# Splitting a group's x one slot sooner, with a wait for each third, in a float32 graph attention kernel

## What is computed

```python
bias = (adj + adj)[:, None]
q = (x @ Wq.T).reshape(b, n, 12, 32); k = (x @ Wk.T)...; v = (x @ Wv.T + bv)...
scores = jnp.einsum('bqhd,bkhd->bhqk', q, k) * 384 ** -0.5 + bias
row_nonzero = jnp.any(scores != 0, axis=-1, keepdims=True)
p = jnp.nan_to_num(softmax(where(row_nonzero, scores, -inf)))
out = einsum('bhqk,bkhd->bqhd', p, v).reshape(b, n, 384) @ Wo.T + bo
result = layernorm(x + out)
```

## Time and profile before

| | us |
|---|---|
| median of 3 runs | 661.67 (661.62 to 662.46) |
| the profiled execution | 661.33 |
| span of its profile | 659.5 |
| PE busy in the span | 638.3 |
| ACT busy | 517.6 |
| DVE busy | 502.6 |
| POOL busy | 410.4 |

### The profile page before, as it was taken

The page is one execution under the profiler, slowest core; times in us unless marked ns, Lnnn a source line. Parts: engine busy times, 40 slices in busy tenths (PEclk is TensorE's granted clock), DMA queues, the critical chain, the costliest instruction groups (busy, mean ns, idle before and its releaser), DMA issues.

```text
span 659.5 us, 18322 instructions
## 1 busy us (share of the span) xinstructions
PE 638.3 (97%) x6060; PEld 550.3 (83%) x6060; DVE 502.6 (76%) x2319; ACT 517.6 (78%) x1942; POOL 410.4 (62%) x500
## 2 busy tenths in 40 slices
PE   9999999999999999999999999999999999999774
PEld 5788888888888888888888888888888888888673
DVE  4667887877887777887877887777877877877884
ACT  5678887878878788877878878788877878877782
POOL 1557665756756666765766856666765756845662
PEclk9999999999999999999999999999999999999999
DMA  9300312121121210212121131210212111011111
GB/s 306 122 4 9 106 57 105 57 74 44 48 105 58 104 50 19 95 59 104 58 86 41 38 106 58 104 50 29 85 58 105 57 50 36 32 58 58 49 49 49
DMA packets 17951, 45.88 MB, mean 70 GB/s; under 512 B 1984, under 2 KB 7104, under 8 KB 17856
## 3 DMA queue, kind: packets, MB, share of 16 engines
q1 hardware_dynamic: 17424, 44.11, 19.3%
q10 hardware_dynamic: 432, 0.59, 0.3%
HBM read 32.11 MB, written 12.58 MB: 68 GB/s over the span
## 4 chain that ended last, share of the span: by engine, by line
PE 67%; POOL 16%; issue 8%; DVE 7%; ACT 2%; POOLq 0%
PE qk_ps L279 21%; PE vo_ps L357 11%; POOL tree L230 10%; PE vo_ps L311 10%; PE pt_ps L325 9%; PE scores_ps L296 6%; PE att_ps L342 5%; DVE nscores L498 4%; POOL x_t L212 4%; PE pt_ps L332 2%; ACT probs L409 2%; PE scores_ps L369 1%; PE pt_ps L265 1%; POOL x_n L219 1%; DVE att_t L538 1%
## 5 line engine op out<-in xcount | busy, mean ns | idle before, releaser
L409 ACT ACTIVATE probs<-nscores,neg_max 128x128 f32<-128x128 f32 x768 | 296.7, 391 | 3.1 <-DVE neg_max L498 3.1
L498 DVE CUSTOM_DVE_ANT_0 nscores<-scores_ps,adj_n 128x128 f32<-128x128 f32 x768 | 171.6, 286 | 16.0 <-PE scores_ps L296 16.0
L409 ACT ACTIVATION_READ_ACCUMULATOR probs<-nscores,neg_max 128x1 f32 x768 | 146.5, 191 | 0.0
L230 POOL TENSOR_TENSOR tree<-nscores 128x768 f32<-128x768 f32 x64 | 120.2, 1878 | 36.0 <-DVE neg_max L498 36.0
L325 PE MATMUL pt_ps<-ident,probs 128*128 128x128 f32 x768 | 118.7, 277 | 9.2 <-ACT probs L409 7.0
L357 PE MATMUL vo_ps<-w_o,att_t 128*128 128x384 f32 x576 | 116.8, 347 | 0.0
L212 POOL TENSOR_TENSOR x_t<-x_raw,x_t 128x512 fp32r<-128x512 f32 x45 | 58.4, 1300 | 93.5 <-ACT x_t L426 93.5
L311 PE MATMUL vo_ps<-w_v,x_t 128*128 128x384 f32 x576 | 114.1, 342 | 0.0
L325 PEld LDWEIGHTS pt_ps<-ident,probs 128*128 128x128 f32 x768 | 89.8, 140 | 28.9 <-ACT probs L409 7.9
L230 POOL TENSOR_TENSOR tree<-tree 128x384 f32<-128x384 f32 (+1 forms) x128 | 103.8, 811 | 10.0
L279 PE MATMUL qk_ps<-x_t,w_k 128*128 128x512 f32 x405 | 105.4, 404 | 2.6 <-POOL x_t L212 2.6
(11 more groups left out here) (56 smaller groups left out, 808.2 us busy)
## 6 DMA issues: line engine op xcount, KB each, us to landing
x_n<-xn SPq DMA_DIRECT2D x32, 384.0 KB, 3.6
out<-out_n SPq DMA_DIRECT2D x32, 384.0 KB, 2.6
x_raw<-xt SPq DMA_DIRECT2D x15, 768.0 KB, 5.4
adj_n<-adj SPq DMA_DIRECT2D x32, 128.0 KB, 2.0
x_raw<-xt SPq DMA_DIRECT2D x3, 256.0 KB, 5.5
nscores<-wq ACTq DMA_DIRECT2D x3, 192.0 KB, 4.2
nscores<-wk SPq DMA_DIRECT2D x3, 192.0 KB, 5.5
probs<-wv SPq DMA_DIRECT2D x1, 576.0 KB, 6.4
```

Of the source, the lines that this page charges most:

```text
L230: nc.gpsimd.tensor_tensor(tree[:, b % 2, :, 0:width], src[:, :, 0:width], src[:, :, width:2 * width], ALU.add).then_inc(tree_step, 1)
L409: last = nc.scalar.activation(probs[:, b % 2, h], nscores[:, b % 2, h], ACT.Exp, bias=neg_max[:, b % 2, h:h + 1], scale=-1.0, accum_out=ro ...
L498: last = nc.vector.tensor_tensor_reduce(out=nscores[:, half, h], in0=scores_ps[j][:, m * P:(m + 1) * P], in1=adj_n[:, b // 2 % 2, half], s ...
```

## The change

`split_in(b)` gives the third that is split at the end of slot b, on ACT and on POOL: third 0 in slot 3, third 1 in slot 0, third 2 in slot 1, and none in slot 2. The group is the same as before, so each third is split one slot sooner; group 2's first third is split in the iteration b = -1. PE's tile 0 waits for one third ahead of each of its three triples of matmuls, in place of one wait for all three ahead of the first.

```diff
+        def split_in(b):
+
+            g, k = (b + 1) // GRP + 2, (b + 1) % GRP
+            return ((g, k),) if k < KT and g < NG else ()
...
-                if 0 <= b and b % GRP < KT and b // GRP + 2 < NG:
-                    split_x_low(b // GRP + 2, b % GRP)
+                for g, k in split_in(b):
+                    split_x_low(g, k)
...
-                if t == 0:
-                    pe.wait_ge(x_split, KT * g)
                 if tile == 0:
                     pe.wait_ge(first_keys, KT)
                 wait(pe, kept, tile)
                 for k in range(KT):
+                    if t == 0:
+                        pe.wait_ge(x_split, KT * (g - 1) + k + 1)
...
-                if 0 <= b and b % GRP < KT and b // GRP + 2 < NG:
-                    split_x_high(b // GRP + 2, b % GRP)
+                for g, k in split_in(b):
+                    split_x_high(g, k)
```

## The result

| | before | changed |
|---|---|---|
| median of 4 runs, us | 661.64 | 655.78 (654.72 to 656.41) |
| the profiled execution, us | 661.33 | 654.72 |
| span, us | 659.5 | 652.9 |

The ratio is 0.9907, with a 95% interval of 0.9890 to 0.9924: 0.9% faster, where 1.0% was forecast. The time lies in the range (654.2 to 656.8).

A forecast was written before the change was run, and what follows sets the result against it. PE was taken as the bound. 661.33 - 6.4 for 14 stalls removed, with nothing for the added waits, gave 654.9 for the profiled execution; the median, 0.34 higher, should be 655.2 us, range 654.2 to 656.8.

The forecast's parts named there:

- The bound: PE, busy 97% of the span, bounds the kernel; a gain must come from its work or its little idling.
- rival 1: Another wait takes the stall's place at tile 0; half the gain goes, 658.5 us; chance 0.05.
- rival 4: POOL's split is held by something other than its place (load or buffer); time stays 661.7 us; chance 0.02.
- part 1: Splits one slot sooner: the stall at slot 3's tile 0 goes wholly, 14 x 0.46 = 6.4 us; lower end 2.7.
- What is late next: After the stall goes, nothing else stands within 0.46 us; the work moved on ACT and POOL costs nothing.
- ACT's cover: ACT's 1.05 us idle at slot 3's end takes the moved 0.62 us high part, leaving 0.43; cost nothing.
- At the start: Group 2's first third added to ACT at b = -1; copy up to 0.1 us late, taken as 0.
- Part 2: Two more waits in each of 15 tiles 0, 30 in all, long satisfied: cost nothing; upper end 6.0 us.
- rival 2: Waits inside tile 0 cost 0.10 us each (658.2 us) or 0.20 (661.2, no change); chance 0.06.
- rival 3: A wait inside tile 0 drains the weight-load pipe, up to 0.43 us each, 668.1 us, slower; chance 0.02.
- The allowance for the differences between runs: Part of the forecast range: 0.8 us, the difference among the three runs shown.
- the 1.2 us kept for the waits: Part of the forecast range: a small price of tile 0's added waits, up to 0.04 us each.

The follow-up runs named there:

- late_before: The kernel before, with POOL making the last third's low part twice (first copy to an unread scratch buffer): 678.67 us, ratio 1.0265.
- late_after: The changed kernel, with POOL making the last third's low part twice (first copy to an unread scratch buffer): 654.77 us, ratio 0.9904.
- late_thirds: The kernel before with tile 0 waiting for each third alone, plus POOL making the last third's low part twice: 661.31 us, ratio 0.9998.
- part 2 alone: The kernel before with splits left in place, but tile 0 waiting for each third alone: 654.90 us, ratio 0.9912.

## Why the prediction was right

**The bound.** That PE is the bound in every slot held to the hundredth: the period after is four slots of pure PE work, 39.01 as forecast, and the delay put in on purpose (late_before) came out in full. The last third is ready at 282.73 in the changed kernel's trace and tile 0's weights start at 291.01, 8.3 us to spare, as forecast. Rivals 1 and 4 are out: the list of PE's waits has no new name, and slot 3 is as long as slot 1.

**The term of part 1.** 14 x 0.46 = 6.4 us against 6.61 in the profiled executions. Of the three readings of a stall (PE's idle 0.19, the weights' idle 0.43, the difference of like slots 0.46) the last was right. PE's own idle figure would have given 2.7 us, 0.27 us too little for each stall. The ends of matmuls are modelled in the profile and overlap in part; that this is why the figure falls short is likely and was not tested.

**What is late next.** Nothing, as forecast. ACT's cover at the new place was 1.05 us and 0.53 of it remain (I had said 0.43); POOL's row sums kept their place with 0.26 us left of 1.29. In late_after the same idle time ahead of slot 2's row sums was used up, and no time was lost. At the start, ACT's split of group 2's first third ran at 28.88 and the copy started at 29.54, where it was at 29.55: nothing, as taken.

**Part 2.** The price of the waits was taken as nothing, and none showed, by 765 of them under 0.001 us each. That refutes rivals 2 and 3 as far as satisfied waits go. An unsatisfied one held back only what stood behind it (late_thirds).

**What I did not see** is that part 2 alone would have removed the stall. I gave the whole gain to part 1 and looked at part 2 only for its cost, though the rows for it were there: the last third came 0.43 us late for the tile's first matmul, but its own first matmul stands some 1.2 us further on. So the sign and size of the forecast did not depend on which part did the work: with either part left out the time would have come out the same.

**The level.** Forecast 655.2, measured 655.78 in the first comparison and 654.84 and 655.11 in two others. A part of the scatter comes from the clock in the last 15 us, which the prediction had not looked at (it read the clock only in the steady slots), and a part from the start. The allowance for the differences between runs, 0.8 us, was thin: the four runs of the first comparison lie 1.7 us apart. That the median still fell into the range owes something to the 1.2 us kept for the waits, which cost nothing.

## What to carry to other kernels

- A stall of a few tenths of a microsecond that repeats is priced best by comparing two stretches with equal work, one with and one without it. On PE the idle time that the profile gives is only a lower end (0.19 us where 0.46 were lost).
- If an operand comes in parts and the consumer takes them in order, a wait for each part cost nothing here when it was satisfied, and hid a producer that was late by less than the parts in front take. Moving the producer a slot ahead did the same and bore 1.23 us more delay for nothing (7.0 us are left by the rows; more delay was not tried). It needs idle time of the engines at the new place.
- Where both remedies are at hand, try each alone: the gain is that of the stall, and is had once.

## What the runs showed of the hardware

- A semaphore wait that is satisfied cost nothing measurable ahead of a matmul (765 more of them: -0.4 us in the medians, -0.1 us in the traces' loops), in the middle of an accumulation too.
- An unsatisfied wait at a block's head cost a little more than the idle time of weight loads (0.43 us idle, 0.46 or 0.47 in the period; 1.65 idle, 1.69 in the slot), one inside a block less (0.48 idle, 0.35 in the period). PE's own idle time at the head was 0.19 and 1.42 us, 0.27 short of the loss both times.
- Behind the same waits of PE at the end (1.32 and 0.88 us), the granted clock fell to the lower level in some executions and not in others; nine matmuls then took 2.90 in place of 1.84 us, and the end of the kernel 1.4 us more.
- The mean granted clock of an execution also counts a fall behind the last matmul: late_after read 0.997 with no matmul at the lower level.
